# Router logits from unsplit tokens on four column groups, in a fused LoRA and mixture-of-experts kernel

## The reference

```python
def cond(x, slot):                       # per sequence: slot picks the adapter
    return x @ W.T + b + 2 * (x @ A[slot]) @ B[slot]
xt = cond(x, itok)                       # 1024 x 512
logits = xt @ router_w + router_b        # 512 -> 16
scores = softmax(logits) + router_bias
# best 2 of 4 groups by their maximum, then the best 2 experts of those
gate = scatter(scores at the 2 experts)
for e in range(16):
    h = silu(xt @ w1[e] + b1[e]) * (xt @ w2[e] + b2[e])      # 512 -> 128
    y += gate[:, e] * (h @ w3[e] + b3[e])                    # 128 -> 512
z = silu(xt @ sw1 + sb1) * (xt @ sw2 + sb2) @ sw3 + sb3      # hidden 256
out = x + y + z
```

## Time and profile before

| | us |
|---|---|
| time before, median of 3 runs | 159.47 (158.26 to 160.37) |
| the profiled execution's own time | 158.81 |
| its span in the trace | 157.0 |

### The profile page before, as it was taken

One profiled execution on the slowest core, in us unless ns is written; L12 is line 12 of the kernel. 1 busy time (PEld: TensorE's weight loads), 2 busy tenths in 40 slices (PEclk: granted clock), 3 DMA queues, 4 the chain that ended last, 5 costly groups with the idle time before them and its releaser, 6 DMA issues.

```text
span 157.0 us, 2751 instructions
## 1 busy us (share of the span) xinstructions
PE 146.0 (93%) x828; PEld 109.9 (70%) x829; DVE 95.4 (61%) x243; ACT 52.5 (33%) x110; POOL 52.2 (33%) x69
## 2 busy tenths in 40 slices
PE   3979999999989999999889999999999998799991
PEld 3857676776857777898676677777776775378760
DVE  1762475188787679979614556654533453368993
ACT  3462152542722261145164333433343332400000
POOL 7720220000000020427225575777566656330000
PEclk9999999999999999999999999999999999999999
DMA  4999978999977699999442456787776799935994
GB/s 147 375 262 361 398 267 262 363 411 414 414 250 289 174 380 357 391 454 336 129 125 69 136 192 209 221 279 256 249 223 244 162 347 342 293 138 187 320 380 182
DMA packets 16669, 43.14 MB, mean 275 GB/s; under 512 B 2224, under 2 KB 2224, under 8 KB 16400
## 3 DMA queue, kind: packets, MB, share of 16 engines
q1 hardware_dynamic: 11392, 25.41, 45.8%
q0 software_dynamic: 3776, 12.59, 25.2%
q10 hardware_dynamic: 1488, 4.98, 8.3%
HBM read 34.06 MB, written 8.91 MB: 274 GB/s over the span
## 4 chain that ended last, share of the span: by engine, by line
PE 69%; DVE 12%; DMA 8%; ACT 5%; issue 3%; SPq 1%; DVEq 0%
PE bank L983 22%; PE bank L1158 20%; PE bank L1176 9%; PE bank L1148 5%; DMA condW_raw<-in_condWT 4%; DMA xg_sb<-xt_rows,slot_tok 4%; DVE x_sb L934 4%; DVE x_sb L947 3%; PE bank L1046 3%; PE bank L1026 2%; DVE x_sb L942 2%; PE bank L1169 2%; PE bank L1036 1%; PE bank L1003 1%; PE bank L1138 1%
## 5 line engine op out<-in xcount | busy, mean ns | idle before, releaser
L1158 PE MATMUL bank<-w_sb,xgT_sb 128*128 x144 | 37.0, 382 | 0.8 <-issue 0.7
L1158 PEld LDWEIGHTS bank<-w_sb,xgT_sb 128*128 128x128 f32 x144 | 25.4, 190 | 11.8 <-issue 9.1
L457 POOL DMA_INDIRECT xg_sb<-xt_rows,slot_tok x22 | 21.3, 968 | 15.6 <-PE bank L1148 6.2
L463 POOL DMA_INDIRECT y_rows<-y_ring,slot_row x18 | 19.6, 1087 | 17.8 <-DVE y_ring L876 17.8
L864 DVE TENSOR_TENSOR pre_sb<-bank,b_sb 128x256 f32<-128x256 f32 x18 | 7.6, 424 | 24.2 <-PE bank L1158 21.9
L1176 PE MATMUL bank<-w_sb,hT_sb 128*128 x36 | 18.5, 595 | 0.6 <-ACT hT_sb L607 0.6
L983 PE MATMUL bank<-condW_h,xT_h 128*128 128x512 f32 x32 | 14.2, 442 | 0.8 <-DVE condW_l L676 0.8
L876 DVE COPY y_ring<-bank 128x512 f32<-128x512 f32 x18 | 12.3, 684 | 1.5 <-issue 1.5
L983 PE MATMUL bank<-xtT_h,sw_h 128*128 128x512 f32 x32 | 13.2, 412 | 0.0
L983 PE MATMUL bank<-condW_l,xT_h 128*128 128x512 f32 x32 | 12.8, 400 | 0.0
L599 ACT COPY xgT_sb<-bank 128x512 f32<-128x512 f32 x18 | 10.6, 587 | 6.5 <-PE bank L1148 5.5
(11 more groups left out here) (168 smaller groups left out, 253.7 us busy)
## 6 DMA issues: line engine op xcount, KB each, us to landing
w_sb<-in_w SPq DMA_DIRECT2D x8, 1024.0 KB, 10.4
w_sb<-in_w ACTq DMA_DIRECT2D x2, 2048.0 KB, 16.1
xt_rows<-xt_ring SPq DMA_DIRECT2D x8, 256.0 KB, 5.0
b_sb<-in_b SPq DMA_DIRECT2D x1, 2048.0 KB
x_sb<-in_x SPq DMA_DIRECT2D x8, 256.0 KB
low_sb<-y_rows SPq DMA_DIRECT2D x4, 512.0 KB
high_sb<-y_rows SPq DMA_DIRECT2D x4, 512.0 KB, 5.6
out<-x_sb SPq DMA_DIRECT2D x8, 256.0 KB, 3.0
```

The costliest lines, as they stand in the source:

```text
L457: pool.indirect_dma_start(xg_sb[:, b % 4, :], None, xt_rows, bass.IndirectOffsetOnAxis(ap=slot_tok[:, b:b + 1], axis=0)).then_inc(gathered ...
L463: pool.indirect_dma_start(y_rows, bass.IndirectOffsetOnAxis(ap=slot_row[:, b:b + 1], axis=0), y_place(b), None).then_inc(y_scattered[b % Y ...
L1158: mm = pe.matmul(bank[2 + s % 2][:, 0:2 * INTER], xgT_sb[:, s % 2, k, :], w12_sb[:, bass.ds(e * W12 + k * 2 * INTER, 2 * INTER)], start=(k ...
```

## The change

The turned tile is first kept whole, in 32 bits, by ACT: `xtT_whole`, two buffers of one tile each. ACT then casts the high part from that copy, after waiting for its own copy, and DVE makes the rest from it. `logits_turned` takes the whole tile and the router weight (high and rest) as 32-bit operands. Quarter k of the depth goes to columns 32k to 32k+31 of PE and so to rows 32k to 32k+31 of bank 6, and nothing is accumulated there; the sum over the four quarters and the two parts is made by `both`, now 128 by 16, in `logits`. `both` is made by POOL's one `affine_select` on `tmp` and a reduction on DVE. PE's waits on `xtT_done` in `turn_xt` and `logits_turned` are now waits on `xt_whole`; `shared_up` waits for `xtT_done` itself. ACT's copy of tile i waits for `lgT_done` and `xtT_done` of the tiles whose buffer it takes over.

`xtT_whole` lies where `sw3_raw` did in stage 1. So SP loads sw3 after w3, when the last `logits_turned` and `lo_xtT` are done, and ACT casts it after `hi_hs(3)` in stage 3 instead of in stage 2.

```diff
--- before.py
+++ after.py
@@ -124,6 +124,7 @@
         hT_sb = at(140, "hT_sb", [P, 2, P])
 
 
+        xtT_whole = at(144, "xtT_whole", [P, 2, KC, P])
         sw3_raw = at(144, "sw3_raw", [P, IC, DIM])
         sw3_split = at(148, "sw3_h", [P, IC, DIM], F32R), at(144, "sw3_l", [P, IC, DIM], F32R)
         xt_ring = at(148, "xt_ring01", [P, 2, DIM]), at(176, "xt_ring23", [P, 2, DIM])
@@ -157,13 +158,13 @@
         slot_no_i = sb("slot_no_i", [P, BPAD], I32)
 
 
-        both = sb("both", [2 * E, E])
+        both = sb("both", [P, E])
         slot_i = sb("slot_i", [P, GROUPS_L], I32)
         slot_f = sb("slot_f", [P, GROUPS_L])
         slot_f2 = sb("slot_f2", [P, GROUPS_L])
         lora_row = sb("lora_row", [P, GROUPS_L], I32)
-        lgT = sb("lgT", [2 * E, 2 * P])
-        rb_col = sb("rb_col", [2 * E, 1])
+        lgT = sb("lgT", [P, 2 * P])
+        rb_col = sb("rb_col", [P, 1])
         lgs = sb("lgs", [P, TILES, E])
         ex = sb("ex", [P, TILES, E])
         sc = sb("sc", [P, TILES, E])
@@ -219,8 +220,8 @@
 
         condW_hi, condW_done, rw_hi, rw_done = sem("condW_hi"), sem("condW_done"), sem("rw_hi"), sem("rw_done")
         xT_hi, xT_done, sw12_hi, sw12_done = sem("xT_hi"), sem("xT_done"), sem("sw12_hi"), sem("sw12_done")
-        loraA_copied, loraB_hi, loraB_done = (
-            sem("loraA_copied"), sem("loraB_hi"), sem("loraB_done"))
+        loraA_copied, both_ready, xt_whole, loraB_hi, loraB_done = (
+            sem("loraA_copied"), sem("both_ready"), sem("xt_whole"), sem("loraB_hi"), sem("loraB_done"))
         lhT_hi, lhT_done, xtT_hi, xtT_done = sem("lhT_hi"), sem("lhT_done"), sem("xtT_hi"), sem("xtT_done")
         pool_step, consts_ready = sem("pool_step"), sem("consts_ready")
         lora_row_ready = sem("lora_row_ready")
@@ -341,7 +342,6 @@
             load_xT(3)
             sp.wait_ge(condW_done, KC)
             sp.dma_start(sw12_raw[:], sw12).then_inc(sw12_in, 16)
-            sp.dma_start(sw3_raw[:], sw3).then_inc(sw3_in, 16)
             load_xT(4)
 
             for i in range(TILES):
@@ -356,6 +356,9 @@
             sp.wait_ge(sw12_done, 2)
             sp.wait_ge(xT_done, XCHUNKS)
             load_experts(sp, 0, E, w3_sb, w3)
+            sp.wait_ge(lgT_done, PAIRS)
+            sp.wait_ge(xtT_done, TILES)
+            sp.dma_start(sw3_raw[:], sw3).then_inc(sw3_in, 16)
 
             sp.wait_ge(sh_up_done, IC)
             sp.dma_start(b12_sb[:], b12.partition_broadcast(P)).then_inc(b12_in, 16)
@@ -398,7 +401,7 @@
             pool.memset(lmask[:], LORA_SCALE).then_inc(pool_step, 1)
             pool.memset(ones[:], 1.0).then_inc(pool_step, 1)
             pool.memset(tri16[:], 1.0).then_inc(pool_step, 1)
-            pool.memset(both[:], 0.0).then_inc(pool_step, 1)
+            pool.memset(tmp[:], 0.0).then_inc(pool_step, 1)
             pool.wait_ge(pool_step, 5)
             pool.affine_select(out=ident[:], in_=ident[:], compare_op=ALU.not_equal, fill=1.0, base=0,
                                pattern=[[-1, P]], channel_multiplier=1).then_inc(consts_ready, 1)
@@ -422,10 +425,8 @@
             pool.wait_ge(lora_row_ready, 1)
             gather_lora(0)
             gather_lora(1)
-            for e in (0, E):
-                pool.affine_select(out=both[:], in_=both[:], compare_op=ALU.not_equal, fill=1.0, base=-e,
-                                   pattern=[[-1, E]], channel_multiplier=1).then_inc(pool_step, 1)
-                pool.wait_ge(pool_step, 8 + e // E)
+            pool.affine_select(out=tmp[:], in_=tmp[:], compare_op=ALU.not_equal, fill=1.0, base=0,
+                               pattern=[[-E, TILES], [-1, E]], channel_multiplier=1).then_inc(pool_step, 1)
             pool.affine_select(out=upper_b[:], in_=ones[:], compare_op=ALU.is_gt, fill=0.0, base=0,
                                pattern=[[1, P]], channel_multiplier=-1).then_inc(consts_ready, 1)
             pool.tensor_copy(ones_b[:], ones[:]).then_inc(consts_ready, 1)
@@ -438,7 +439,7 @@
 
             pool.wait_ge(logits_done, PAIRS)
             pool.memset(gate[:], 0.0).then_inc(pool_step, 1)
-            pool.wait_ge(pool_step, 10)
+            pool.wait_ge(pool_step, 9)
             pool.memset(gate[:, :, E:E + 1], 1.0).then_inc(gate_ones, 1)
             pool.memset(gate[:, :, 32 + E:32 + E + 1], 1.0).then_inc(gate_ones, 1)
             by_block = [P, K * TILES, BPAD]
@@ -519,8 +520,12 @@
             def hi_xtT(i):
                 act.wait_ge(xt_turned, i + 1)
                 n, t = i * P // HALF, i * P % HALF
-                act.copy(xtT_split[n][0][:, :, t:t + P],
-                         bank[2 + i % 2][:].rearrange("p (k t) -> p k t", k=KC)).then_inc(xtT_hi, 1)
+                if i >= 2:
+                    act.wait_ge(lgT_done, i // 2)
+                    act.wait_ge(xtT_done, i - 1)
+                act.copy(xtT_whole[:, i % 2], bank[2 + i % 2][:].rearrange("p (k t) -> p k t", k=KC)).then_inc(xt_whole, 1)
+                act.wait_ge(xt_whole, i + 1)
+                act.copy(xtT_split[n][0][:, :, t:t + P], xtT_whole[:, i % 2]).then_inc(xtT_hi, 1)
 
             def exps(q):
                 tiles = slice(2 * q, 2 * q + 2)
@@ -530,7 +535,7 @@
             def copy_lgT(q):
 
                 act.wait_ge(lgT_done, q + 1)
-                act.activation(lgT[:], bank[6][0:2 * E, 0:2 * P], ACT.Identity, bias=rb_col[:, 0:1]).then_inc(lgT_copied, 1)
+                act.activation(lgT[:], bank[6][:, 0:2 * P], ACT.Identity, bias=rb_col[:, 0:1]).then_inc(lgT_copied, 1)
 
             for k in (0, 1, 3):
                 act.dma_start(condW_raw[:, k, :], condWT[k]).then_inc(condW_in[k], 16)
@@ -587,8 +592,6 @@
             hi_hs(1)
             for s in range(2):
                 act.wait_ge(xt_stored[s], 16 * TILES // XT_RING)
-            act.wait_ge(sw3_in, 16)
-            act.copy(sw3_split[0][:], sw3_raw[:]).then_inc(sw3_hi, 1)
             hi_hs(2)
             act.wait_ge(b3s_in, 16)
             act.copy(b3s_split[:], b3s_raw[:]).then_inc(b3s_hi, 1)
@@ -619,6 +622,8 @@
                 act.copy(gateT[:, n * 512:(n + 1) * 512], bank[4 + n][0:STACK, :]).then_inc(gateT_copied, 1)
             silu(0, 0)
             hi_hs(3)
+            act.wait_ge(sw3_in, 16)
+            act.copy(sw3_split[0][:], sw3_raw[:]).then_inc(sw3_hi, 1)
             act.wait_ge(eid_ready, 1)
             top = last_group(act)
             left = blocks_left(act)
@@ -703,8 +708,7 @@
             def lo_xtT(i):
                 dve.wait_ge(xtT_hi, i + 1)
                 n, t = i * P // HALF, i * P % HALF
-                rest(xtT_split[n][1][:, :, t:t + P], bank[2 + i % 2][:].rearrange("p (k t) -> p k t", k=KC),
-                     xtT_split[n][0][:, :, t:t + P], xtT_done)
+                rest(xtT_split[n][1][:, :, t:t + P], xtT_whole[:, i % 2], xtT_split[n][0][:, :, t:t + P], xtT_done)
 
             lg = bank[6][:, 2 * P:3 * P].rearrange("p (i e) -> p i e", e=E)
 
@@ -745,6 +749,9 @@
             lo_lora(0)
             dve.wait_ge(consts_ready, 5)
             mask_lh(0)
+            dve.wait_ge(pool_step, 8)
+            dve.tensor_reduce(both[:], tmp[:].rearrange("p j e -> p e j"), AX.X, ALU.add).then_inc(both_ready, 1)
+            dve.wait_ge(both_ready, 1)
             dve.wait_ge(small_in, 16 * 5)
             dve.tensor_copy(rw_split[:, :, 0, :], rw_raw[:]).then_inc(rw_hi, 1)
             dve.wait_ge(rw_hi, 1)
@@ -1031,36 +1038,37 @@
             def turn_xt(i):
                 pe.wait_ge(xt_ready, i + 1)
                 if i >= 2:
-                    pe.wait_ge(xtT_done, i - 1)
+                    pe.wait_ge(xt_whole, i - 1)
                 for k in range(KC):
                     mm = pe.transpose(bank[2 + i % 2][:, k * P:(k + 1) * P], xt_place(i)[:, k * P:(k + 1) * P], ident[:])
                 mm.then_inc(xt_turned, 1)
 
             def logits_turned(q):
-                pe.wait_ge(xtT_done, 2 * q + 2)
+                pe.wait_ge(xt_whole, 2 * q + 2)
                 if q >= 1:
                     pe.wait_ge(shifted, q)
-                n, t = 2 * q * P // HALF, 2 * q * P % HALF
-                for k in range(KC):
-                    for part in range(2):
-                        mm = pe.matmul(bank[6][0:2 * E, 0:2 * P], rw_split[:, k].rearrange("p m e -> p (m e)"),
-                                       xtT_split[n][part][:, k, t:t + 2 * P],
-                                       start=(k == 0 and part == 0), stop=(k == KC - 1 and part == 1))
+                for i in range(2):
+                    for k in range(KC):
+                        mm = pe.matmul(bank[6][k * COLS:(k + 1) * COLS, i * P:(i + 1) * P],
+                                       rw_split[:, k].rearrange("p m e -> p (m e)").bitcast(F32), xtT_whole[:, i, k, :],
+                                       start=True, stop=True)
                 mm.then_inc(lgT_done, 1)
 
             def logits(q):
 
                 if q == 0:
-                    pe.wait_ge(pool_step, 9)
+                    pe.wait_ge(both_ready, 1)
```

(6 more changed lines are left out.)

## The result

The changed kernel takes 162.28 us (median of 4 runs, 161.82 to 163.77) against 158.87 us for the kernel before, run beside it (median of 4 runs, 157.31 to 160.37). The medians lie 3.4 us apart. The ratio is 1.027, 95% interval 1.021 to 1.033, which is some 4.2 us; ratios and intervals here leave out an execution that is over 1.5% above the fastest of its kernel, in this case the 160.37. Forecast were 162.5 us and +3.4 us. The time is right, but two terms of the sum are not, and neither is the time from which the forecast starts, as the rows and the later runs show.

The account below looks back on a forecast made before the run. PE sets most of the time, except ACT-DVE-PE chains at odd tiles and the first gather behind q1. Gather's turn 2.7 plus sw3's cast 0.7 make +3.4 us: 162.5 us, range 160.0 to 164.0.

Parts of the forecast that it names:

- a = 0.65 us: Stage 1, ACT: copying the whole turned tile before its cast adds 0.65 us per tile, eight times; could be 0.48 to 0.75.
- ACT's copy is covered: Rival, stage 1: ACT's copy is off the chain and costs nothing; sum +0.8 us, 159.6 to 160.3 us; chance 15%.
- g = 0.40 us: Stage 1, PE: logits product takes 0.54 us instead of 0.94, saving 0.40 us per pair of tiles; ends 0.26 and 0.50.
- The 0.08 for changing: Logits product, PE: estimated 0.08 us to change to column groups, counted only in the saving's lower end of 0.26 us.
- 4a - 3g = 1.36: Stage 1, bias of tile 7: four copy costs less three product savings, less a few hundredths, make it 1.36 us later.
- The step of 1.6 to the counts: After tile 7: DVE's choices come late, PE waits for them, and counts and first gather's issue shift by 1.6 us.
- The fourth saving: Last pair's logits product: PE waits for DVE's choices before the counts anyway, so the faster product gains nothing there.
- sw3 in the queue, 1.33 us: Queue q1 before the first gather: sw3's 0.52 MB take 1.33 us at 395 GB/s; the drain, 2.7 us later, decides.
- ACT's cast of sw3 ... +0.7 us: First block, stage 3: the cast delays ACT's copy of `hT_sb` and PE's first down product by 0.7 us; 0 to 0.95.
- Sharing of the queues: Rival, first gather: it alternates with q1, so moves only with its issue; sum +2.3 to +2.5, 161.1 to 162.0 us; 20%.
- The clock: Sign of error: PE's granted clock, full in all stretches before, falls in the new pause before the first block; no size given.
- +2.4 to +4.2: Whole kernel: the sum's range in us, said to come from the ends of copy, product saving and both sw3 terms.

Follow-up runs that it names:

- sw3 early: Changed kernel with sw3 loaded and cast where the kernel before does it, whole tiles in other free buffers: 160.77 us, 1.0145 times the kernel before.
- old product, sw3 early: Changed kernel with sw3 loaded and cast in its old place and the logits product again from the split parts; ACT's copy stays: 161.47 us, 1.0194 times before.
- only the cast late: Kernel before with one edit: ACT casts sw3 after `hi_hs(3)` at the first block, sw3 still loaded early: 158.86 us, 1.0040 times before.
- the load late too: Kernel before with both moves of sw3: loaded behind w3 and cast at the first block: 159.65 us, 1.0094 times before.
- the reordered pair: Changed kernel with ACT's high-part cast after x^T's or sw12's and DVE's rest a pass later: sw3 in its old place 157.81 us, sw3 late 159.80 us.

## Why the prediction was right, and where it was not

Shifts against the trace of before, counted from the turn of tile 0 (us; the forecast's are its own):

| | forecast | changed kernel | sw3 early | old product, sw3 early |
|---|---|---|---|---|
| turn of tile 1 | 0.65 | 0.60 | 0.60 | 0.60 |
| turn of tile 3 | 0.90 | 1.05 | 1.07 | 1.26 |
| turn of tile 5 | 1.14 | 1.46 | 1.48 | 1.90 |
| turn of tile 7 | 1.2 | 1.73 | 1.76 | 2.40 |
| counts | 1.6 | 2.01 | 2.05 | 3.17 |
| turn of the first block | 2.7 | 3.63 | 1.35 | 2.50 |
| first down product | 3.4 | 5.27 (with the fall of the clock, 1.64) | 1.30 | 2.45 |

The last two rows stand against the slow gather of the trace before. Against the trace with only the cast late the turn of the first block is shifted by 4.3, 2.0 and 3.2 us.

- **The copy, a = 0.65 us: right.** 0.66 and 0.64 in the version that has the copy alone, and no cover for it anywhere: the rival "ACT's copy is covered" falls.
- **The product, g = 0.40 us: mis-sized, the mechanism right.** g measured 0.19 to 0.23, below the lower end of 0.26. "I take 0.54 us" for the product was nearly met (0.57). What the sum lacked is its entry: the first product starts 0.10 us later behind the product ahead, and turning the adapter behind it takes 0.49 instead of 0.44. The 0.08 for changing, which no row gives, was put into an end of g only, and its reason, the column groups, was wrong as well: it comes with one group too.
- **4a - 3g = 1.36 for the bias of tile 7:** with g = 0.2 it is 2.0. The bias comes 1.88 us later in the changed kernel (52.29 against 50.96, counted from tile 0), and PE's turn 1.73, with most of the reserve of 0.2 that was counted. The step of 1.6 to the counts was 2.0.
- **The fourth saving worth nothing: right.** PE is done with the last pair's product early (55.00 to 55.58 in the changed kernel) and DVE's choices set the counts. What the forecast did not see is what the new product gives there against the old one: it does not wait for the rest of tile 7. In the version with the old product PE stands 0.69 us for it, and the counts come 3.17 - 2.05 = 1.1 us later, more than the three savings; the turn of the first block moves with them, by 2.50 - 1.35 = 1.15:

```profile
56.46 0.31 PE L1053 MATMUL bank<-xtT_h,rw_split 128*32 128x256 f32 x1 [0.69 <-DVE xtT_l L681]
```

- **sw3 in the queue, 1.33 us: right, and the drain decides.** The gather's first packet, counted from tile 0, moves by 1.34 us from the version with only the cast late to that with the load late too (52.75 to 54.09), by 1.33 in the reordered pair (51.81 to 53.14) and by 1.53 from sw3 early to the changed kernel (54.61 to 56.14). In all thirteen traces it comes when q1 runs out, 1.8 to 3.9 us after the issue. Against the kernel before (52.79) it is 3.35 us later, where 2.7 were forecast; 0.5 of the rest is g. The landing is a less sure measure: from its first packet to PE's turn the gather takes 2.9 to 4.3 us in these traces, 2.9 with only the cast late, 3.5 before and 3.8 in the changed kernel. The forecast has no term for that, and no run shows what sets it.
- **"ACT's cast of sw3 ... +0.7 us": this step failed.** The cast adds 0.2. The step added the cast's length to the time of the copy that follows. But the gap of 0.67 us ahead of that copy is gone once the cast stands ahead of ACT's register loads, and PE had 0.47 us between the end of the copy and the down product.
- **Sharing of the queues: it did not happen while q1 was full.** From 71.13 to 75 the gather moved nothing, and of two versions that issue it at the same time (69.59 and 69.66) the one with more bytes in q1 lands it 1.4 us later, where this rival had it land with its issue. In 73.1 to 73.5, which the prediction takes from the earlier trace rows, both queues do move (q0 has 40 packets in 73.0 to 73.5), but that is q1's end. The Trainium skill (DMA: Bandwidth & Descriptors, section Queues, rings and completion order) says that an engine goes round-robin over queues that have work; for this gather behind q1 no trace shows such turns. Whether its packets already lay in the queue and were passed over, or got there late, no row shows.
- **The clock:** named among what would prove the prediction wrong, and it did fall in the profiled execution, by 1.64 us. In most executions it does not.
- **The ends, "+2.4 to +4.2":** they are those of a and g alone (2.45 and 4.25). With the cast's own ends, 0 and 0.95, the sum runs from +1.8 to +4.5.

That the time came out right is in part luck, since errors cancel. In the sum the cast was over-counted by 0.5 us, and three savings by 3 x 0.2 = 0.6 in the other direction; the longer flight of the gather, 0.3 us against the trace before and 0.9 against the one with only the cast late, was not forecast. And the base was too high: the forecast adds its 3.4 to 159.1, while the kernel before has medians of 158.2 to 158.3 in the three larger sets beside the experiments. With a difference of 4.2 that leads to the same 162.5.

In medians, from versions that differ by one part: the copy +3.1, the product -0.7, sw3's place +1.8 by one pair and, with both its moves, +1.5 on the kernel before. These were measured at different times and each is uncertain by 0.5 us or more. The sum is near +4.2 by the first and +3.9 by the second; measured were +4.2 by the ratio, both times (1.027 and 1.0266). The +3.4 between the first two medians comes from a kernel before whose four executions had a median of 158.87. The copy alone shows 3.1 and not 4a = 2.6 because of that wait for the rest of tile 7, which the new product takes away again. Of sw3's price the queue has 1.3 to 1.5 us and the cast 0.2. How much of the rest is the gather's flight and how much the clock stays open.

## What to carry to other kernels

A faster product is worth what the engine that feeds it does not lose: 0.36 us saved within the product per pair, 0.2 of it left after its late start, was paid for with 0.65 us per tile on ACT, in a chain that had no reserve. If a change frees a step from a dependency, move that step too: the same change with the cast and the rest moved behind x^T's cast was 3 us faster than without that, and the first version to beat the kernel before. And a buffer borrowed from a load has the load's new place as its price: 0.52 MB put ahead of a gather in a full queue delayed its first packet by 1.3 to 1.5 us, more than the product gave (0.7 us in time).

## What the runs showed of the hardware

- Whole 32-bit products on a 32-column tile start 0.32 to 0.33 us after a product of 512 columns, and their weights are not loaded ahead of it (0.36 to 0.37 us idle of the weight loads); split products on the same size of tile start after 0.23 us, with the weights loaded ahead. The Trainium skill (TensorEngine Tiling (Array Packing), section Tiling Modes) says that changing the tiling mode drains TensorE. The split product changes between the same two tile sizes without that delay, so here the tile size alone does not bring it.
- Four column groups of 32-bit products with 128 columns: 0.57 us for 16 instructions, against 1.86 us in one group (3.2 times). 8 instructions of 256 columns take the same 0.57 us.
- A gap of 0.67 us ahead of ACT's copy `hT_sb`, where its register loads stand, was gone when a cast of 1.04 us stood ahead of them; the copy came only 0.2 us later.
- A gather issued while q1 is full moves its first packet when q1 runs out, 1.8 to 3.9 us after the issue, and PE turns its rows 2.9 to 4.3 us after that packet.
- The granted clock fell to its lower level in single executions after pauses of PE: once ahead of the first block (after 2.16 us) and in two executions in stage 1 (after 0.88 and 0.52 us, and after 0.90 and 0.51), 1.5 to 1.6 us each. In the version with only the cast late it fell after pauses of 0.44, 0.52 and 0.47 us near 138 us (0.50 in 138 to 140). The version with sw3 early has pauses of 0.90 and 0.52 us in stage 1 too and kept the full clock there.
